# Output projection in four uses of one token tile, projection products regrouped, small exponential moved

## The chip, the cores and the metric

The kernel runs on one core of a Trainium2 chip. The metric is the device time of one execution in microseconds, as the median of several runs. TensorE (PE) multiplies, ScalarE (ACT) computes Ln and Exp, VectorE (DVE) does the elementwise work and the copies out of PSUM, GpSimd (POOL) only fills constants at the start, SyncE (SP) issues the DMAs. PSUM has eight banks of 128 x 512 fp32.

## The reference

One transformer layer on x of shape (8, 1024, 256), fp32, with 16 heads of 16 columns. Cut to what matters:

```python
xn = layernorm(x)
q, k, v = heads(xn @ Wq.T), heads(xn @ Wk.T), heads(xn @ Wv.T)
q, k, v = exp_map(q), exp_map(k), exp_map(v)        # tanh(|v|) * v / |v|
arg  = max(1 + 2c * |q_i - k_j|^2 / ((1 - c|q_i|^2) (1 - c|k_j|^2)), 1 + eps)
w    = softmax(-beta * arccosh(arg) / sqrt(c), axis=-1)
o    = log_map(exp_map(w @ log_map(v)))
x    = x + concat(o) @ Wo.T
y    = layernorm(x) quantised to e4m3, @ kernel quantised to e4m3, in fp32
x    = x + (bf16(y) + bias)
```

## The kernel before

**Tiling.** The 8192 tokens are 16 groups G of 512 tokens (4 tiles of 128), two groups to a batch entry. For each query group the attention runs over 4 head groups of 4 heads and 8 key tiles: 32 steps s of one chunk, 512 steps in all. A chunk is 128 keys x 4 heads x 512 queries. In a step PE makes the distance products of the chunk (L1100, 8 matmul instructions a step, half of chunk n+1 and half of chunk n+2), ACT takes Ln of the chunk in PSUM (L1217) and Exp of the one before (L1224), PE multiplies the values by the weights (L1115). In the loop the order on ACT is Ln(n), Exp(n-1), and after them, in one step of a group, the small exponential (L529, 128x128) for the projection. The distance products have two halves of a ring in six PSUM banks; those for chunk n+1, second half, wait until Ln(n) has emptied its banks (semaphore `freed`), and Ln(n+1) waits for them (`d_rdy`).

**Open units.** For each unit of 4 chunks a flag says whether some distance may reach the bound 1/eps. Where it is set, DVE first writes the bounds (L1285) and multiplies them into the distances (L1294), and ACT takes Ln of that (L1212). With these inputs three units are open: steps 4 to 7 of group 5, 20 to 23 of group 8, 12 to 15 of group 15.

**Side work in bank 7.** The other work runs beside the attention, in one PSUM bank (7), one use after another: PE fills it, DVE copies it out, and only then may PE fill it again (`b7_filled`, `b7_copied`). Uses of the projection of a coming group: X 0, 1 (x transposed), M 0 to 7 (products with Wq, Wk, Wv, two for a token tile, 128x384), R 0 to 7 (rows of q and k transposed), A 0, 1 (largest value over the tokens, transposed twice; the opens flags come from it). Uses of the finish of a group whose attention is over: T 0, 1 (attention output transposed), W (output projection), Q (quantised rows transposed), Y 0, 1 (second product). S turns the sums of a head group and DVE normalises them (`normalise`, L1308 to L1312), in steps 2, 10, 18 and 26 of a group.

**The order.** It is written out by hand. `PROJECT_USES` and `FINISH_USES` give each use a slot and a half: 0 is whole ahead of the products with the values, 1 whole behind them, `BOTH` a half ahead and a half behind. The projection of group n, from 3 on, runs in group n-2 with slot k at step k-4 (`EARLY`), the finish of group n in group n+1 with slot k at step k. Group 2 (`SECOND_USES`), group 1 (`FIRST_USES`) and the finish of group 14 (`SHORT_USES`, `SHORT_SLOTS`, in group 15) have tables of their own. The functions `vector`, `scalar` and `sync` of both stages hold, by slot, the work of DVE, ACT and SP. On every engine the instructions stand in one queue in this order. In a step DVE first does the copies of the step's uses, then the vector slots of the finish and of the projection. In a step with no use of bank 7 PE multiplies a constant into it instead (L1138, `keep_busy`, two instructions ahead of the values and two behind); the step `BARE` has neither.

**Names of the slots before.** Projection: squares and their sums in slots 9, 11, 14, 17; reciprocal roots by Newton steps (L267 to L269) in 18 and 19, at the end of 19 `nrm` (L596); values scaled in 20; the small exponential in 21 (ACT) and its use in 21 to 23 (DVE); rows scaled (L554) in 24. Finish: slots 3 to 8 for the output's length, 21 and 22 for mean and variance of the layernorm, 23 to 26 normalising and quantising, 28 and 32 the rest; SP loads x in slot 2 and stores the result in slot 33.

Of the kernel before, what the change touches and what calls it, by code (L numbers as in the profile page):

```python
# [303 lines left out]
def project_stage(nc, ctx, g, a, uses):  # L304


    def sb(name, shape, dt=F32):
# [222 lines left out]

    def first_vector(v, n, step):
# [7 lines left out]
        vector(v, n, 18, step)  # L539
        vector(v, n, 19, step)  # L540
        if n == 0:
            v.wait_ge(zeroed, ZEROED)
        vector(v, n, 20, step)
        vector(v, n, 21, step)
        vector(v, n, 22, step)
# [1084 lines left out]
```

## Time and profile before

| what | value |
|---|---|
| median of 3 runs | 1992.58 us (1991.73 to 1993.07) |
| profiled execution, its own time | 1994.49 us |
| its span, first to last instruction | 1992.7 us |
| busy: ACT / PE / DVE | 1869.9 us (94%) / 1788.6 us (90%) / 1142.9 us (57%) |
| Ln of closed chunks (L1217) | x500, mean 1911 ns, idle before 35.5 us, of it 31.6 waiting for PE L1100 |
| Exp (L1224) | x512, mean 1949 ns, idle before 0.3 us |
| Ln of open chunks (L1212) | x12, idle before 28.4 us, of it 28.3 waiting for DVE L1294 |
| mean granted clock of PE | 0.972 of full speed |

Busy times overlap: ACT's instructions are listed with a part of their wait in its queue, so start times tell more than durations. Clock 1 means that PE ran at its upper level, 2.4 GHz.

### The profile page before, as it was taken

How to read it: one execution, taken by the hardware profiler on the slowest of the kernel's cores; microseconds unless marked ns; L12 is line 12 of the kernel's file. 1: busy time of each engine (PE TensorE's matmuls, PEld its weight loads, DVE VectorE, ACT ScalarE, POOL GpSimd, SP SyncE). 2: the span in 40 equal slices, each digit the busy share in tenths (PEclk: the TensorE clock that was granted, in tenths of full speed). 3: DMA queues.
4: the chain of work that ended last, by engine and by line, in shares of the span. 5: the costliest groups of instructions: out<-in, count | busy, mean ns of one | idle time of the engine just before them, and what ended most of it. 6: DMA issues, size and time to landing. Idle time of an engine off the chain costs nothing.

```text
span 1992.7 us, 29554 instructions
## 1 busy us (share of the span) xinstructions
PE 1788.6 (90%) x10713; PEld 603.1 (30%) x10713; DVE 1142.9 (57%) x2825; ACT 1869.9 (94%) x1094; POOL 12.8 (1%) x35
## 2 busy tenths in 40 slices
PE   7988989989898798989998898998989899899897
PEld 4322222323232232322322223232322223233234
DVE  7454565655656656565656647565565656323436
ACT  4889999999999799999998999999999999999883
POOL 2000000000000000000000000000000000000000
PEclk9799999999999899999999899999999999999889
DMA  1314213141312213132040321314131131411110
GB/s 56 112 49 144 54 54 103 42 134 43 112 44 78 77 44 112 43 101 75 23 134 22 110 67 44 112 43 134 40 107 52 56 90 43 123 43 53 33 33 23
DMA packets 112953, 142.54 MB, mean 72 GB/s; under 512 B 35691, under 2 KB 61548, under 8 KB 112748
## 3 DMA queue, kind: packets, MB, share of 16 engines
q1 hardware_dynamic: 112748, 140.13, 22.6%
q8 instruction: 89, 1.46, 0.3%
q14 instruction: 116, 0.95, 0.2%
HBM read 85.07 MB, written 55.05 MB: 70 GB/s over the span
## 4 chain that ended last, share of the span: by engine, by line
ACT 54%; PE 24%; issue 14%; DVE 4%; ACTq 3%; DMA 0%; DVEq 0%; SPq 0%
ACT U L1217 28%; ACT U L1224 26%; PE ps L1100 8%; PE ps L401 6%; PE ps L1115 5%; ACTq L1265 2%; PE ps L695 2%; DVE U L1294 1%; PE ps L1138 1%; PE ps L406 1%; PE ps L1142 1%; DVE U L1285 1%; DVE rows L554 0%; DMA U<-in_L_attn_W_o_dram 0%; ACT e L529 0%
## 5 line engine op out<-in xcount | busy, mean ns | idle before, releaser
L1224 ACT ACTIVATE U<-U 128x2048 f32<-128x2048 f32 x512 | 997.1, 1949 | 0.3
L1217 ACT ACTIVATE U<-ps 128x2048 f32<-128x2048 f32 x500 | 955.7, 1911 | 35.5 <-PE ps L1100 31.6
L1100 PE MATMUL ps<-q_T,k_T 18*128 18x512 f32 x4096 | 632.5, 652 | 133.0 <-ACT U L1217 107.7
L1115 PE MATMUL ps<-U,vals 128*32 128x512 f32 x4096 | 560.4, 620 | 29.4 <-ACT U L1224 28.9
L1100 PEld LDWEIGHTS ps<-q_T,k_T 18*128 18x128 f32 x4096 | 195.9, 187 | 356.8 <-ACT U L1217 296.4
L401 PE MATMUL ps<-wT,xnT 128*128 128x384 f32 x512 | 232.0, 545 | 4.9 <-DVEq L1318 2.5
L490 DVE COPY qkv<-ps 128x384 f32<-128x384 f32 x112 | 62.4, 557 | 243.7 <-PE ps L401 243.6
L1115 PEld LDWEIGHTS ps<-U,vals 128*32 128x32 f32 x4096 | 81.7, 109 | 205.4 <-ACT U L1224 159.2
L401 PEld LDWEIGHTS ps<-wT,xnT 128*128 128x128 f32 x512 | 81.1, 194 | 197.0 <-issue 132.4
L1138 PE MATMUL ps<-woT,ident 128*128 128x256 f32 x340 | 121.8, 441 | 3.8 <-DVEq L1318 3.6
L406 PE MATMUL ps<-ident,rows 128*128 128x128 f32 x512 | 107.2, 308 | 4.9 <-DVE rows L554 2.4
L406 PEld LDWEIGHTS ps<-ident,rows 128*128 128x128 f32 x512 | 55.1, 146 | 176.4 <-issue 114.5
L1138 PEld LDWEIGHTS ps<-woT,ident 128*128 128x128 f32 x340 | 52.0, 193 | 145.2 <-issue 116.0
L1300 DVE COPY OTs<-ps 128x512 f32<-128x512 f32 x64 | 43.8, 684 | 88.0 <-PE ps L1115 75.3
L498 DVE COPY q_T<-ps 128x512 f32<-128x512 f32 x60 | 41.5, 691 | 90.9 <-PE ps L406 90.3
L500 DVE COPY k_T<-ps 128x512 f32<-128x512 f32 x60 | 41.5, 691 | 62.8 <-PE ps L406 60.8
L695 PE MATMUL ps<-woT,fi_ocT 128*128 128x256 f32 x240 | 68.6, 409 | 0.0
L1308 DVE TENSOR_REDUCE den<-ps 128x16 f32<-128x256 f32 x64 | 27.2, 424 | 58.2 <-PE ps L1124 57.2
L695 PEld LDWEIGHTS ps<-woT,fi_ocT 128*128 128x128 f32 x240 | 41.0, 191 | 51.8 <-issue 37.3
L723 DVE TENSOR_TENSOR fi_x<-fi_xt,ps 128x512 f32<-128x512 f32 x30 | 20.6, 688 | 61.9 <-PE ps L695 61.9
L587 DVE TENSOR_TENSOR sqr<-qkv 128x768 f32<-128x768 f32 x56 | 53.3, 953 | 2.4
L588 DVE TENSOR_REDUCE ss<-sqr 128x48 f32<-128x768 f32 x56 | 53.4, 953 | 1.9
(209 smaller groups left out, 1179.6 us busy)
## 6 DMA issues: line engine op xcount, KB each, us to landing
rqb<-q_scratch SPq DMA_DIRECT2D x64, 1024.0 KB, 5.6
q_scratch<-q_T SPq DMA_DIRECT2D x16, 1024.0 KB, 4.5
k_scratch<-k_T SPq DMA_DIRECT2D x16, 1024.0 KB, 6.8
v_scratch<-vals SPq DMA_DIRECT2D x16, 768.0 KB, 9.6
fi_xt<-in_L_attn_x_dram SPq DMA_DIRECT2D x17, 512.0 KB, 6.0
xt<-in_L_attn_x_dram SPq DMA_DIRECT2D x15, 512.0 KB, 6.7
out_dram<-fi_x SPq DMA_DIRECT2D x15, 512.0 KB, 4.6
rk_scratch<-rk SPq DMA_DIRECT2D x16, 32.0 KB, 12.5
```

Of the source, the lines that this page charges most:

```text
L401: ins = pe.matmul(bank[:, 0:384], xnT[:, dc, t * P:(t + 1) * P], g.wT[:, dc, half * 384:(half + 1) * 384], start=dc == 0, stop=dc == 1)
L406: ins = pe.transpose(bank[:, t * P:(t + 1) * P], rows[:, qk, t, hg * HPG:(hg + 1) * HPG, :].rearrange("p h r -> p (h r)"), g.ident[:, :])
L490: v.tensor_copy(qkv[:, t, 24 * half:24 * (half + 1), :].rearrange("p h d -> p (h d)"), bank[:, 0:384]).then_inc(a.b7_copied, 1)
L587: step(v.tensor_tensor(sqr[:, :], src, src, ALU.mult))
L588: step(v.tensor_reduce(ss[:, t, :], sqr[:, :].rearrange("p (h d) -> p h d", d=DH), AX.X, ALU.add))
L695: ins = pe.matmul(bank[:, a * D:(a + 1) * D], ocT[:, dc, t * P:(t + 1) * P], g.woT[:, dc, :], start=dc == 0, stop=dc == 1)
L1100: ins = pe.matmul(g.ps[:, 2 * pair + i, :], a.k_T[HB * h:HB * h + RD, b % 2, hg, kt * P:(kt + 1) * P], a.q_T[HB * h:HB * h + RD, G % 3, hg ...
L1115: ins = pe.matmul(g.ps[HB * h:HB * h + VW, 6, :], a.vals[:, b % 2, kt, (hg * HPG + h) // 2, DH * (h % 2):DH * (h % 2) + VW], U[:, n % RING ...
L1138: pe.matmul(g.ps[:, 7, 0:D], g.ident[:, :], g.woT[:, 0, :], start=True, stop=True)
L1217: act.activation(U[:, n % RING].rearrange("p b n -> p (b n)"), chunk(n), ACT.Ln, scale=-2.0 / EPS, bias=1.0).then_inc(freed, 1)
L1224: act.activation(U[:, n % RING], U[:, n % RING], ACT.Exp, scale=exponent).then_inc(exp_done, 1)
L1300: v.tensor_copy(OTs[:, :], g.ps[:, 6, :]).then_inc(ot_done, 1)
```

## The change

1. Output projection: W 0 and W 1, each with two token tiles, become W 0 to W 3 with one tile each (slots 15, 16, 17, 19). The residual addition is by one tile, and `bn_stats` follows tile by tile in the same slots.
2. The products M 0 to M 7 of groups from 3 on: slots 7, 8, 9, 10, 12, 13, 15, 16 become 7, 8, 10, 11, 12, 15, 16, 17. T 0 moves from 13 to 9.
3. The Newton steps are spread over slots 19, 20, 21 (`nrm` at the end of 21), the small exponential moves from slot 21 to 22 on ACT, what uses it from 21, 22, 23 to 23, 24, 25, the scaling of the rows from 24 to 25 (q) and 26 (k), the values' scaling from 20 to 35 (31 for group 2).
4. R and A move by one slot; A 0, A 1 and R 4 are new in the second half of slots 28, 31 and 30. Steps S and R in the tables of groups 1 and 2 no longer share step 10, and R 0 of group 2 stands in the second half of step 26.
5. The stores of q, k, v, rk go from slot 34 to 36, the output's from 33 to 34. The finish of group 14 uses the common table with the slots packed from step 10 on.
6. `BARE` is step 5 instead of 7.

```diff
-PROJECT_SLOTS = 35
-FINISH_SLOTS = 34
+PROJECT_SLOTS = 37
+FINISH_SLOTS = 35
 PROJECT_USES = {("X", 0): (4, BOTH), ("X", 1): (5, BOTH),
-                ("M", 0): (7, BOTH), ("M", 1): (8, BOTH), ("M", 2): (9, BOTH), ("M", 3): (10, BOTH),
-                ("M", 4): (12, BOTH), ("M", 5): (13, BOTH), ("M", 6): (15, BOTH), ("M", 7): (16, BOTH),
-                ("R", 0): (25, BOTH), ("R", 1): (26, BOTH), ("R", 2): (27, 0), ("A", 0): (27, 1),
-                ("R", 3): (28, BOTH), ("R", 4): (29, BOTH), ("R", 5): (31, 0), ("A", 1): (31, 1),
+                ("M", 0): (7, BOTH), ("M", 1): (8, BOTH), ("M", 2): (10, BOTH), ("M", 3): (11, BOTH),
+                ("M", 4): (12, BOTH), ("M", 5): (15, BOTH), ("M", 6): (16, BOTH), ("M", 7): (17, BOTH),
+                ("R", 0): (26, BOTH), ("R", 1): (27, BOTH), ("R", 2): (28, BOTH), ("A", 0): (28, 1),
+                ("R", 3): (29, BOTH), ("R", 4): (30, 1), ("R", 5): (31, BOTH), ("A", 1): (31, 1),
                 ("R", 6): (32, BOTH), ("R", 7): (33, BOTH)}
-FINISH_USES = {("T", 0): (13, BOTH), ("T", 1): (14, BOTH), ("W", 0): (15, BOTH), ("W", 1): (17, BOTH),
+FINISH_USES = {("T", 0): (9, BOTH), ("T", 1): (14, BOTH), ("W", 0): (15, BOTH), ("W", 1): (16, BOTH),
+               ("W", 2): (17, BOTH), ("W", 3): (19, BOTH),
                ("Q", 0): (30, BOTH), ("Y", 0): (31, 0), ("Y", 1): (31, 1)}
-SHORT_USES.update({("Q", 0): (28, BOTH), ("Y", 0): (30, 0), ("Y", 1): (30, 1)})
-BARE = 7
-SHORT_SLOTS = {23: (23, 24), 24: (25, 26), 25: (27, 28), 26: (29,), 27: (30, 31), 28: (32,), 29: (33,), 30: (), 31: ()}
+BARE = (5,)
+SHORT_SLOTS = {10: (10, 11, 12, 13), 11: (14,), 12: (15,), 13: (16,), 14: (17, 18), 15: (19,), 16: (20, 21), 17: (22,),
+               18: (23,), 19: (24,), 20: (25,), 21: (26, 27), 22: (28, 29, 30), 23: (31, 32), 24: (33,), 25: (34,),
+               26: (), 27: (), 28: (), 29: (), 30: (), 31: ()}
 FIRST_USES = {("A", 0): (2, 0), ("R", 4): (2, 0), ("A", 1): (2, 0), ("R", 5): (3, BOTH), ("R", 6): (6, BOTH),
-              ("R", 7): (11, BOTH), ("R", 0): (14, BOTH), ("R", 1): (17, BOTH), ("R", 2): (19, BOTH),
-              ("R", 3): (20, BOTH)}
+              ("R", 7): (14, BOTH), ("R", 0): (17, BOTH), ("R", 1): (19, BOTH), ("R", 2): (20, BOTH),
+              ("R", 3): (21, BOTH)}
-SECOND_USES.update({("R", 0): (25, BOTH), ("R", 1): (26, BOTH), ("R", 2): (27, 0), ("A", 0): (27, 1), ("R", 3): (28, 0),
-                    ("R", 4): (28, 1), ("R", 5): (29, BOTH), ("R", 6): (30, 0), ("A", 1): (30, 1), ("R", 7): (31, BOTH)})
+SECOND_USES.update({("M", 2): (9, BOTH), ("M", 4): (12, BOTH), ("M", 5): (13, BOTH), ("M", 6): (15, BOTH), ("M", 7): (16, BOTH),
+                    ("R", 0): (26, 1), ("R", 1): (27, 0), ("A", 0): (27, 1), ("R", 2): (28, 0), ("R", 3): (28, 1),
+                    ("R", 4): (29, BOTH), ("R", 5): (30, 0), ("A", 1): (30, 1), ("R", 6): (31, 0), ("R", 7): (31, 1)})
...
         elif kind == "W":
-            for a in halves(part, range(2)):
-                t = 2 * i + a
-                for dc in range(2):
-                    ins = pe.matmul(bank[:, a * D:(a + 1) * D], ocT[:, dc, t * P:(t + 1) * P],
-                                    g.woT[:, dc, :], start=dc == 0, stop=dc == 1)
+            for dc in halves(part, range(2)):
+                ins = pe.matmul(bank[:, 0:D], ocT[:, dc, i * P:(i + 1) * P], g.woT[:, dc, :],
+                                start=dc == 0, stop=dc == 1)
...
     def scalar(act, n, k):
-        if k == 21:
+        if k == 22:
...
-        if k == 19:
-            newton(v, step, ss[:, :, :], y[:, :, :], y2[:, :, :], 2)
+        if k == 20:
+            newton(v, step, ss[:, :, :], y[:, :, :], y2[:, :, :], 1)
+        if k == 21:
+            newton(v, step, ss[:, :, :], y[:, :, :], y2[:, :, :], 1)
             v.tensor_tensor(nrm[:, :, :], ssqk, yqk, ALU.mult).then_inc(n_rdy, 1)
...
-        if k == 21:
-            v.wait_ge(b7_copied, uses.after(("W", n, 1)))
-            for t in range(GT):
-                step.mark(v.bn_stats(stats[:, t, :], x1[:, t, :]))
+        if k in (15, 16, 17, 19):
+            t = {15: 0, 16: 1, 17: 2, 19: 3}[k]
+            v.wait_ge(b7_copied, uses.after(("W", n, t)))
+            step.mark(v.bn_stats(stats[:, t, :], x1[:, t, :]))
+        if k == 20:
```

## Rows read from the trace of the kernel before

**Rows 1.** Timeline of group 3 and the first step of group 4, ACT: start, us, what.

```profile
415.58 1.96 ACT L1217 ACTIVATE U<-ps 128x2048 f32<-128x2048 f32 x1
419.13 1.97 ACT L1217 ACTIVATE U<-ps 128x2048 f32<-128x2048 f32 x1
...
437.06 1.88 ACT L1217 ACTIVATE U<-ps 128x2048 f32<-128x2048 f32 x1
...
440.82 1.88 ACT L1217 ACTIVATE U<-ps 128x2048 f32<-128x2048 f32 x1
...
530.71 1.97 ACT L1217 ACTIVATE U<-ps 128x2048 f32<-128x2048 f32 x1
```

**Rows 2.** Timeline, group 3, steps 15 to 18; in brackets the idle time before.

```profile
473.12 1.88 ACT L1217 ACTIVATE U<-ps 128x2048 f32<-128x2048 f32 x1
...
475.77 1.14 PE L1100 MATMUL ps<-q_T,k_T 18*128 18x512 f32 x8
...
476.94 1.88 ACT L1217 ACTIVATE U<-ps 128x2048 f32<-128x2048 f32 x1
...
479.09 1.14 PE L1100 MATMUL ps<-q_T,k_T 18*128 18x512 f32 x8
...
480.51 0.39 ACT L529 ACTIVATE e<-nrm,sc 128x128 f32<-128x128 f32 x1
...
480.81 1.87 ACT L1217 ACTIVATE U<-ps 128x2048 f32<-128x2048 f32 x1
```

**Rows 3.** Timeline, group 3, steps 23 and 24: A 0 and transpositions.

```profile
502.26 1.90 ACT L1217 ACTIVATE U<-ps 128x2048 f32<-128x2048 f32 x1
...
503.74 0.28 PE L411 MATMUL ps<-ident,amax 128*32 128x128 f32 x1 [0.23 <-DVE q_T L498]
...
504.21 1.24 PE L1100 MATMUL ps<-q_T,k_T 18*128 18x512 f32 x8 [0.19 <-ACT U L1217]
...
507.48 0.69 DVE L498 COPY q_T<-ps 128x512 f32<-128x512 f32 x1 [1.61 <-PE ps L406]
```

**Rows 4.** Timeline, DVE, group 3 and the last tokens of the kernel.

```profile
478.49 0.36 DVE L269 SCALAR_TENSOR_TENSOR y<-y 128x192 f32<-128x192 f32 x1
...
478.89 0.29 DVE L596 TENSOR_TENSOR nrm<-ss,y 128x128 f32<-128x128 f32 x1
...
1966.76 0.42 DVE L886 TENSOR_TENSOR fi_x<-fi_xt,ps 128x256 f32<-128x256 f32 x1 [0.70 <-PE ps L842]
1967.21 0.43 DVE L887 BATCH_NORM_STATS2 fi_stats<-fi_x 128x6 f32<-128x256 f32 x1
```

**Rows 5.** Timeline, group 3, step 26: the sums.

```profile
514.78 0.49 DVE L1312 TENSOR_TENSOR on<-ps,den 128x128 f32<-128x128 f32 x2
514.91 1.24 PE L1100 MATMUL ps<-q_T,k_T 18*128 18x512 f32 x8 [0.70 <-ACT U L1217]
```

**Rows 6.** ACT's waits in 98:180, 1855:1872 and 1925:1950: us, times, longest.

```profile
ACT U L1217 <- PE ps L1100: 9.7, 3, 5.9
...
ACT U L1217 <- PE ps L1100: 3.7, 2, 2.7
...
ACT U L1217 <- PE ps L1100: 4.0, 3, 1.9
```

**Rows 7.** Timeline, group 8, ahead of its open unit.

```profile
1075.60 1.88 ACT L1217 ACTIVATE U<-ps 128x2048 f32<-128x2048 f32 x1
...
1081.69 1.67 DVE L1285 TENSOR_SCALAR U<-rqb,rk 128x512 f32<-128x512 f32 x4
```

**Rows 8.** Windows: length, busy PE, PEld, DVE, ACT, POOL, granted clock, DMA.

```profile
400.00:500.00 100.00, 92.45 (x572) 29.75 (x571) 57.95 (x141) 99.70 (x57) 0.00 (x0) 1.00 0.27 88
```

**Rows 9.** Timeline, PE, three places with idle time.

```profile
102.94 1.65 PE L401 MATMUL ps<-wT,xnT 128*128 128x384 f32 x2 [2.50 <-DVEq L1318]
...
1855.80 1.81 PE L1100 MATMUL ps<-q_T,k_T 18*128 18x512 f32 x8 [0.70 <-ACT U L1217]
...
1954.19 1.07 PE L1115 MATMUL ps<-U,vals 128*32 128x512 f32 x8 [1.44 <-ACT U L1224]
```

More of the change, by code:

```diff
@@ L366, in sync @@
             sp.dma_start(xt[:, :, :], g.x_g[n + 1]).then_inc(x_in, 16)
-        if k == 34:
+        if k == 36:
             b, u = n // 2, n % 2
@@ L538, in first_vector @@
         step(v.tensor_scalar(ss[:, :, :], ss[:, :, :], EPS * EPS, None, ALU.max))
[L539 to L545, printed above, removed]
+        for k in (19, 20, 21, 35):
+            if k == 35 and n == 0:
+                v.wait_ge(zeroed, ZEROED)
+            vector(v, n, k, step)
+        vector(v, n, 23, step)
+        vector(v, n, 24, step)
         if n == 1:
             v.wait_ge(p_filled, len(FIRST_FILLS))
-        vector(v, n, 23, step)
+        vector(v, n, 25, step)
         scale_rows(v, n, (1, 0) if n == 0 else (1,))
@@ L582, in vector @@
             ins.then_inc(xn_rdy, 1)
-        if k in (9, 11, 14, 17):
-            t = {9: 0, 11: 1, 14: 2, 17: 3}[k]
+        if k in (9, 12, 16, 18):
+            t = {9: 0, 12: 1, 16: 2, 18: 3}[k]
             v.wait_ge(a.b7_copied, uses.after(("M", n, 2 * t + 1)))
@@ L590, in vector @@
                 step(v.tensor_scalar(ss[:, :, :], ss[:, :, :], EPS * EPS, None, ALU.max))
-        if k == 18:
+        if k == 19:
             root_guess(v, step, ss[:, :, :], y[:, :, :])
             newton(v, step, ss[:, :, :], y[:, :, :], y2[:, :, :], 1)
-        if k == 19:
-            newton(v, step, ss[:, :, :], y[:, :, :], y2[:, :, :], 2)
+        if k == 20:
+            newton(v, step, ss[:, :, :], y[:, :, :], y2[:, :, :], 1)
+        if k == 21:
+            newton(v, step, ss[:, :, :], y[:, :, :], y2[:, :, :], 1)
             v.tensor_tensor(nrm[:, :, :], ssqk, yqk, ALU.mult).then_inc(n_rdy, 1)
-        if k == 20:
+        if k == (31 if n == 2 else 35):
+            step = first or Steps(v, g_steps, 2 * (n - 2))
             step(v.tensor_scalar(vg[:, :, :], y[:, :, 2 * H:], g.ZS, 1.0, ALU.mult, ALU.min))
@@ L607, in vector @@
                                 ALU.mult).then_inc(v_rdy, 1)
-        if k == 21:
+        if k == 23:
             v.wait_ge(e_rdy, n + 1)
@@ L621, in vector @@
             step(v.reciprocal(rp[:, :, :], a4[:, :, :]))
-        if k == 23:
+        if k == 25:
             if n >= 4:
@@ L629, in vector @@
             v.tensor_reduce(amax[:, :], a4[:, :, :].rearrange("p t h -> p h t"), AX.X, ALU.max).then_inc(amax_rdy, 1)
-        if k == 24:
-            scale_rows(v, n, (1, 0))
-        assert first or step.n == OWN.get(k, 0), (k, step.n)
+            if n >= 2:
+                scale_rows(v, n, (0,))
+        if k == 26:
+            scale_rows(v, n, (1,))
+        assert first or k in (31, 35) or step.n == OWN.get(k, 0), (k, step.n)
     p = Shared()
@@ L670, in sync @@
             if n >= 1:
-                sp.wait_ge(steps_v, PER * (n - 1) + sum(count for slot, count in OWN.items() if slot <= 28))
+                sp.wait_ge(steps_v, PER * (n - 1) + sum(count for slot, count in OWN.items() if slot <= 27))
             sp.dma_start(xt[:, :, :], g.x_g[n]).then_inc(f_in, 16)
-        if k == 33:
+        if k == 34:
             sp.wait_ge(res_rdy, n + 1)
@@ L722, in copy @@
                     v.wait_ge(res_out, 16 * n)
-            v.tensor_tensor(x1[:, two, :].rearrange("p t d -> p (t d)"),
-                            xt[:, two, :].rearrange("p t d -> p (t d)"), bank, ALU.add).then_inc(b7_copied, 1)
+            v.tensor_tensor(x1[:, i, :], xt[:, i, :], bank[:, 0:D], ALU.add).then_inc(b7_copied, 1)
         elif kind == "Q":
@@ L962, in in_step @@
                     found.append(("S", x // HG, x % HG))
-            found += [(kind, n, i) for n, k in finished(G, s) for kind, i in at(finish_uses(n), k, half)]
+            found += [(kind, n, i) for n, k in finished(G, s) for kind, i in at(FINISH_USES, k, half)]
             found += [(kind, n, i) for n, k in projected(G, s) for kind, i in at(project_uses(n), k, half)]
@@ L1054, in _ @@
                 project.first_sync(sp, 2)
-                project.sync(sp, 0, 34)
+                project.sync(sp, 0, 36)
                 load_rq(0)
@@ L1061, in _ @@
                     if n == 21:
-                        project.sync(sp, 1, 34)
+                        project.sync(sp, 1, 36)
                     if n == N - 3:
@@ L1163, in _ @@
                     both = [(kind, m, i) for m, k in projected(G, s) for kind, i in begun(project_uses(m), k)]
-                    both += [(kind, m, i) for m, k in finished(G, s) for kind, i in begun(finish_uses(m), k)]
+                    both += [(kind, m, i) for m, k in finished(G, s) for kind, i in begun(FINISH_USES, k)]
                     if G == 0:
@@ L1172, in _ @@
                         use(*key, 0)
-                    unused = n > 2 and s != BARE and not in_step(G, s, 0) + in_step(G, s, 1)
+                    unused = n > 2 and s not in BARE and not in_step(G, s, 0) + in_step(G, s, 1)
                     if unused:
```

28 lines of the change are left out of this document (12 added, 16 removed).

## The prediction

> **What bounds the kernel now.** I read the page first, for who is busy and who ends the waits, then the timeline of ScalarE (ACT) alone, taking differences of start times, since the listed durations overlap and grow while its queue is full. In the page ACT is the bound: 512 Ln and 512 Exp, and the wait it has most is for the distance products, 31.6 us of the run (the table above). In the timeline, step 96 (group 3, step 0) starts at 415.58 and step 128 at 530.71 [rows 1]: 115.13 us for 32 steps. Unhindered steps start 3.555 apart (415.58 and 419.13); thirty-two of them are 113.8, so a steady group loses only 1.4 us. Over the run 512 x 3.555 = 1820 us; the rest of the 1992.7 us span is what lies ahead of and behind the loop, 14 x 1.4 us in groups 1 to 14, and waits in group 0, in group 15 and in the three units whose flag is open. The profiled execution took 1994.49 us, 1.8 over its span; the median of the runs is 1992.58. I add differences to the median.
>
> Where do the 1.4 us go? The reader should see in [rows 2] how PE's lateness reaches ACT: PE starts a step's distance products at 475.77 and the next Ln starts at 476.94, 1.17 later. It can't start them before the Ln of that step is through, 1.95 us after its start (502.26 and 504.21, where PE waited for just that) [rows 3]. That leaves 3.56 - 1.95 - 1.17 = 0.44 us by which PE may be late for nothing. The use of the output projection in step 111 makes PE start its next products 2.65 us after the Ln (473.12, 475.77) [rows 2]: the allowance is used up, and the next Ln comes 3.82 us after the last (473.12, 476.94) instead of 3.56. The small exponential adds 0.30: 480.51 to 480.81. In a run of four projection products each step past the second is 3.76 long (437.06 to 440.82) [rows 1]: 0.2 lost in each.
>
> **The change, part by part.** Steps are s, slots k; for the projection of a later group s = k - 4, for the finish s = k.
>
> *Output projection in four.* A half of a use is now two instructions of 256 columns instead of four, like the filler's half. The filler step is 475.77 to 479.09, 3.32 us [rows 2], under 3.56: no loss. Gain 0.3 us a group. The additions are four of 0.42 us on DVE [rows 4] instead of two of twice the width, hidden by its idle half, as are the statistics that move with them.
>
> *Products in pairs.* Runs of 4, 2, 2 become 2, 3, 3. By 0.2 for each past the second: 0.4 before, 0.4 after. Nothing. The fullest DVE slot (the copy of R 0, the ten small operations of slot 22, one scaling) comes to a little over a step but is followed by a lighter one: nothing.
>
> *The small exponential.* Its input nrm moves from slot 19 to 21, it only from 21 to 22. So one step lies between them where two did. DVE's slot s=17 now holds: the addition of W 2, which can begin some 5.4 us after the Ln of 17 (a copy behind half a transposition begins 5.22 after the Ln of its step, 502.26 to 507.48 [rows 3]; half a W is 0.2 longer); addition and hand-over 0.45, statistics 0.35, three Newton operations of 0.40 (478.49 to 478.89 is one), nrm 0.29 [rows 4]. Sum 7.7. ACT reaches the exponential 3.57 after the Ln of its step [rows 2], which is 7.13 after the Ln of 17. It waits 0.6 us, and every Ln queued behind it too. Bounds: 0 if DVE is 0.6 quicker than its rows, 1.0 if the copy meets a late PE.
>
> *A 0 behind R 2, A 1 behind R 5.* Both use the same bank. Before, R 2 was whole in the first half and the products with the values lay between. Now R 2 ends in the second half and A 0 can't start until DVE has copied it, 0.69 and a hand-over of 0.06. With the copy at 507.48 A 0 would start at 508.23, end 0.28 later (as at 503.74), and the distance products would start at 508.51; the Ln after them at 509.68 instead of 505.81 + 3.56 = 509.37 (505.81 is 502.26 + 3.55): 0.3 us [rows 3]. A 1 stands the same way behind R 5: 0.3. Bounds 0 and 0.75 each.
>
> *R 4 behind the sums.* In s=26 the sums are turned first, DVE normalises, R 4 stands behind the values. In [rows 5] PE is through with the values at 514.2 (0.70 ahead of 514.91), but DVE with the last of the normalising at 515.3 (514.78 + 0.49) and a hand-over of 0.1: the quantising work of slot 25 held it, and that stays. So PE idles 1.2 us, R 4 takes some 0.6, and the distance products start near 516.0 instead of 514.9: 1.1 late less the allowance of 0.44. Cost 0.7, bounds 0.3 and 0.9.
>
> So groups 1 to 13 get 0.6 + 0.3 + 0.3 + 0.7 - 0.3 = 1.6 us each, 21 us.
>
> *What moves without cost.* The values are scaled at slot 35 (s=31), where DVE had only the copies of Y, and first used at step 4 of the next group, so four steps in hand. The four stores of q, k, v, rk go out at slot 36 (s=0 of the next group) instead of 34; on SP's queue stand behind them the two loads of x, wanted more than ten steps later, and the broadcast load at the next s=4, whose data only open units read. The output store moves one step, to s=2, and its wait for the result holds up the same queue by less than a step. If that cover were gone, each late step of SP would cost 3.6 us once.
>
> *Group 0.* The sums no longer share s=10 with M 3, nor s=26 with a transposition ahead of the values. These were ACT's waits of 5.9 and 3.8, together 9.7 us [rows 6]. Gone but for 0.7: -9.
>
> *Group 15.* Finish of group 14 ends four steps earlier: Q no longer waits for a late DVE; 4.0 us [rows 6]. The step without filler moves from 7 to 5; behind it the clock fell, 3.7 us [rows 6], though the same step of group 14 brought no wait; I count two thirds of it, 2.4. Against it, W 0 to W 3 now fall in the open unit, where DVE is the bound: 3 x 0.5 more. Sum -5.
>
> *Open units.* In group 8 DVE began the bounds of the first open chunk 6.1 us after the Ln of step 275 (1075.60, 1081.69) [rows 7]. Now W 3 is copied there only at 5.45 and 3.0 us of work follow: +2.4. Group 5 -0.5, group 14 -0.4 (W).
>
> Sum without the clock: 21 - 9 - 5 + 1.5 = +8.5 us: 2001.
>
> **The clock.** This decides the size. PE had its upper level, 2.4 GHz, all through 400 to 500 [rows 8]. Elsewhere it fell to 1.2 GHz, and ahead of that PE had idled: 2.50 us in one piece ahead of 102.94 (behind it two product instructions take 1.65 us) [rows 9], and twice in one step ahead of 1855.80, 0.70 us the second time, where the eight distance instructions take 1.81 us [rows 9] instead of the 1.14 at 475.77 [rows 2]. In steady groups there are idle pieces of 0.70 as well, one in a step of the sums [rows 5], and it did not fall [rows 8]. In one place 1.44 us of idle left it up (the values at 1954.19 still take 1.07) [rows 9]. The change makes, in each of groups 1 to 13, one idle of 0.7 (step of the sums) + 0.3 (exponential) + 0.6 (its wait) = 1.55 us at s=18 to 19, one of 1.2 at s=26, and two of 0.75. By the three rows (2.50 fell, 1.44 did not, 0.70 twice in a step fell) I take it to fall about once a group. A fall costs 3.7, 3.8 (of the 9.7) and 4.0 us in [rows 6], part of it the wait that led to it, already counted: 3.0. 13 x 3.0 = 39. Bounds: none, and two falls a group, 78.
>
> The Trainium skill (TensorE: Matmul & The Clock Gate, "A second HAM failure mode: psum-queue depth-cycling") says that short idles between groups of matmuls, often enough, make the clock swing between its levels; by that rule alone every group would fall, by the steady rows alone (0.70 us idle, no fall) none.
>
> Forecast: 1992.6 + 8.5 + 39 = 2040 us.
>
> **The rivals.**
> A. Clock falls once in most groups: 2040, from 2018 (0.45 falls a group) to 2070 (1.7). Chance 0.5.
> B. Waits come, clock stays: 2001 (1996 to 2012). For it: 1.44 us without a fall, and single pieces of 0.70 harmless throughout. Against: 1.55 is longer than any piece that is known to leave it up. Chance 0.25.
> C. Faster: the four waits are mostly covered, that is the exponential's input is ready in time and DVE frees the bank within PE's 0.44 us. Then the groups give 13 x -0.3, with group 0 and 15: -4 -9 -5 +1.5 = -16, 1976; with a third of the waits left 1984. It decides below 0.9 us of waits a group (13 x 0.9 = 12, less the 12.5 gained elsewhere). For it: DVE is busy only 58 of 100 us [rows 8], so its slots may end earlier than the sums say. Against: each wait is a sum of hand-overs that the trace shows. Chance 0.17.
> D. No visible change, gains and losses cancelling, 1989 to 1997: 0.08.
>
> **How the numbers follow.** 0.2% is 4 us, about what a measurement of this kernel can tell. Slower: A 0.5, B 0.24 = 0.74. Same: D 0.08 and a sliver of B, 0.09. Faster: C 0.17. The range goes from 1990, into the cases where the gains win, to 2065, short of two falls in every group: it leaves out most of C and the top of A, 0.2.
>
> **What would show it.** Small exponential: in groups 1 to 13 ACT's wait for nrm 0.6 us at s=18, so 13 such waits in the chain of waits; none refutes that step. A 0, A 1: PE waiting 0.75 for DVE's copies; R 4: PE waiting about 1.1 for the normalising. Steps of W at 3.56 apart. Granted clock: mean well below 0.97, with about 13 stretches at the lower level in groups 1 to 13, most behind s=18; if it stays 0.97 or more, B or C. Group 0: no wait of 5.9 near step 12. Group 15: no wait at Q. The prediction is wrong if the groups are no longer than 115.1 us, which the starts of every 32nd Ln show.

## The result, and the profile after

The changed kernel takes 2031.37 us (median of 6 runs, 2022.14 to 2037.63) where the kernel before takes 1992.15 (6 runs, 1986.07 to 1993.07): ratio 1.0201, 95% interval 1.0175 to 1.0228. It is 39 us slower; 2040 was forecast. The profiled execution took 2031.51 us with a span of 2029.7 us, 37.0 more than the span before. Its mean granted clock is 0.959 (0.972 before).

I read it as before: starts of Ln on ACT. Timeline of group 3 after, its first step and that of group 4:

```profile
409.06 1.89 ACT L1218 ACTIVATE U<-ps 128x2048 f32<-128x2048 f32 x1
...
525.73 1.89 ACT L1218 ACTIVATE U<-ps 128x2048 f32<-128x2048 f32 x1
```

116.67 us where it was 115.13 [rows 1]: 1.54 more; 1.6 was forecast. Group 6 is just as long; in these two the clock stays up. The waits after, of ACT and then of PE (total us, times, longest):

```profile
ACT U L1218 <- PE ps L1101: 53.3, 56, 4.6
...
ACT e L531 <- DVE nrm L599: 9.3, 14, 1.7
```

```profile
PE ps L408 <- DVEq L1319: 17.8, 14, 1.7
...
PE ps L413 <- DVE q_T L500: 14.3, 13, 1.5
PE ps L416 <- DVE k_T L502: 11.2, 15, 0.8
```

All four forecast waits are there: e for nrm, R 4 behind the sums (L408 for DVE's queue), A 0 (L413), A 1 (L416). In the timeline after, group 3, steps 18 and 19:

```profile
473.65 1.89 ACT L1218 ACTIVATE U<-ps 128x2048 f32<-128x2048 f32 x1
...
477.92 0.40 ACT L531 ACTIVATE e<-nrm,sc 128x128 f32<-128x128 f32 x1 [0.58 <-DVE nrm L599]
478.23 1.86 ACT L1218 ACTIVATE U<-ps 128x2048 f32<-128x2048 f32 x1
...
480.14 1.24 PE L1101 MATMUL ps<-q_T,k_T 18*128 18x512 f32 x8 [1.68 <-ACT U L1218]
```

ACT stands 0.58 us for nrm; Ln follows Ln after 4.58, 1.02 over a free step, of which 0.32 was there before. PE then has idled 1.68 us in one piece. Steps 25 to 29 of the same group:

```profile
499.57 1.91 ACT L1218 ACTIVATE U<-ps 128x2048 f32<-128x2048 f32 x1
...
502.16 0.28 PE L413 MATMUL ps<-ident,amax 128*32 128x128 f32 x1 [0.96 <-DVE q_T L500]
...
503.54 1.88 ACT L1218 ACTIVATE U<-ps 128x2048 f32<-128x2048 f32 x1 [0.27 <-PE ps L1101]
...
507.12 1.86 ACT L1218 ACTIVATE U<-ps 128x2048 f32<-128x2048 f32 x1
...
509.62 0.66 PE L408 MATMUL ps<-ident,rows 128*128 128x128 f32 x4 [1.28 <-DVEq L1319]
...
511.39 1.88 ACT L1218 ACTIVATE U<-ps 128x2048 f32<-128x2048 f32 x1 [0.60 <-PE ps L1101]
511.65 1.07 PE L1116 MATMUL ps<-U,vals 128*32 128x512 f32 x8
...
513.87 0.18 PE L416 MATMUL ps<-ident,amax_r 32*1 32x32 f32 x1 [0.79 <-DVE k_T L502]
...
515.05 1.88 ACT L1218 ACTIVATE U<-ps 128x2048 f32<-128x2048 f32 x1
```

A 0 costs 503.54 - 499.57 - 3.555 = 0.42, R 4 costs 511.39 - 507.12 - 3.555 = 0.71, A 1 costs 515.05 - 511.39 - 3.555 = 0.11. (These two are much the same in all quiet groups, but for 1.09 behind R 4 in group 10; A 0 costs between 0.22 and 1.06 in groups 1 to 13.) Now the same place in group 7:

```profile
1001.38 1.88 ACT L1218 ACTIVATE U<-ps 128x2048 f32<-128x2048 f32 x1 [0.60 <-PE ps L1101]
1001.64 1.90 PE L1116 MATMUL ps<-U,vals 128*32 128x512 f32 x8
...
1007.07 1.88 ACT L1218 ACTIVATE U<-ps 128x2048 f32<-128x2048 f32 x1 [2.01 <-PE ps L1101]
```

Steps 26 and 27 lose the same as in group 3 (0.02 and 0.71 us), but here the values take 1.90 us where they took 1.07: the clock has fallen. The next Ln comes 5.69 after the last. The windows after (groups 9 to 13, then group 15; the columns are those of [rows 8], the granted clock is third from the end) say it in sum:

```profile
1156.90:1753.56 596.66, 535.72 (x3249) 167.81 (x3248) 342.05 (x851) 576.09 (x326) 0.00 (x0) 0.97 0.24 74
1867.39:1988.09 120.70, 107.22 (x626) 35.15 (x624) 58.33 (x125) 111.58 (x63) 0.00 (x0) 0.96 0.14 45
```

Before, groups 9 to 13 took 575.86 us at 1.00 and group 15 took 125.22 at 0.89 (up to the last Ln).

**Where the 37 us come from**, by the starts of every 32nd Ln, before and after: group 0 ends at 185.28 and 173.45 (-11.8: it is 9.7 shorter, 137.96 and 128.22, and its first Ln 2.1 earlier, 47.32 and 45.23); groups 1 to 13 together +54.9, that is 13 x 1.54 = 20.0, the first step of group 8's open unit +3.5, and the other 31, which stand in the groups where the clock falls; group 14 -0.9; group 15 -4.5. Sum +37.7; behind the last Ln 0.7 comes back.

Outside the open units the granted clock falls 14 times in groups 1 to 13 after, and never before: once at step 19 or 20 in groups 2, 4, 5, 7, 11, 12 and 13, and at steps 28 to 30 once in groups 7, 8, 9, 11 and 12 and twice in 13. (A fall here is a stretch at the lower level, 1.2 GHz.) 31 / 14 = 2.2 us each.

### The profile page after: what moved, and what is told of

Read it like the earlier page. It is cut to its first block, busy times and chain, and to the rows that moved or that the text cites. A ratio compares the mean times of both kernels' runs of the same rounds, so it can differ in the third digit from the quotient of the medians.

```text
span 2029.7 us, 29437 instructions
## 1 busy us (share of the span) xinstructions
PE 1795.7 (88%) x10645; PEld 588.3 (29%) x10645; DVE 1144.3 (56%) x2855; ACT 1873.5 (92%) x1094; POOL 12.5 (1%) x35
## 4 chain that ended last, share of the span: by engine, by line
ACT 34%; PE 33%; DVE 17%; issue 12%; ACTq 2%; DVEq 1%; DMA 0%; SPq 0%
ACT U L1218 18%; ACT U L1225 16%; PE ps L1101 11%; PE ps L1116 9%; PE ps L403 7%; PE ps L408 2%; PE ps L699 2%; ACTq L1266 2%; DVE q_T L500 2%; DVE rows L555 1%; DVE U L1295 1%; DVE fi_ocT L775 1%; DVE fi_xb L767 1%; DVEq L1365 1%; DVE rp L615 1%
## 5 line engine op out<-in xcount | busy, mean ns | idle before, releaser
L1225 ACT ACTIVATE U<-U 128x2048 f32<-128x2048 f32 x512 | 989.3, 1934 | 0.3
L1101 PE MATMUL ps<-q_T,k_T 18*128 18x512 f32 x4096 | 638.8, 657 | 128.8 <-ACT U L1218 91.5
L1116 PE MATMUL ps<-U,vals 128*32 128x512 f32 x4096 | 571.4, 631 | 19.0 <-ACT U L1225 17.4
L403 PE MATMUL ps<-wT,xnT 128*128 128x384 f32 x512 | 227.9, 537 | 1.6 <-ACT xnT L464 1.6
L408 PE MATMUL ps<-ident,rows 128*128 128x128 f32 x512 | 112.4, 315 | 35.9 <-DVEq L1319 17.8
L408 PEld LDWEIGHTS ps<-ident,rows 128*128 128x128 f32 x512 | 55.4, 148 | 230.9 <-issue 124.1
L727 DVE TENSOR_TENSOR fi_x<-fi_xt,ps 128x256 f32<-128x256 f32 x60 | 25.3, 421 | 127.7 <-PE ps L699 127.7
L1139 PE MATMUL ps<-woT,ident 128*128 128x256 f32 x272 | 96.9, 439 | 0.0
L699 PE MATMUL ps<-woT,fi_ocT 128*128 128x256 f32 x240 | 89.6, 457 | 0.0
L1139 PEld LDWEIGHTS ps<-woT,ident 128*128 128x128 f32 x272 | 41.3, 191 | 113.7 <-issue 101.8
L1213 ACT ACTIVATE U<-U 128x2048 f32<-128x2048 f32 x12 | 22.9, 1911 | 36.5 <-DVE U L1295 36.5
```

What stands on the lines that cost most here:

```text
L403: ins = pe.matmul(bank[:, 0:384], xnT[:, dc, t * P:(t + 1) * P], g.wT[:, dc, half * 384:(half + 1) * 384], start=dc == 0, stop=dc == 1)
L408: ins = pe.transpose(bank[:, t * P:(t + 1) * P], rows[:, qk, t, hg * HPG:(hg + 1) * HPG, :].rearrange("p h r -> p (h r)"), g.ident[:, :])
L699: ins = pe.matmul(bank[:, 0:D], ocT[:, dc, i * P:(i + 1) * P], g.woT[:, dc, :], start=dc == 0, stop=dc == 1)
L1101: ins = pe.matmul(g.ps[:, 2 * pair + i, :], a.k_T[HB * h:HB * h + RD, b % 2, hg, kt * P:(kt + 1) * P], a.q_T[HB * h:HB * h + RD, G % 3, hg ...
L1116: ins = pe.matmul(g.ps[HB * h:HB * h + VW, 6, :], a.vals[:, b % 2, kt, (hg * HPG + h) // 2, DH * (h % 2):DH * (h % 2) + VW], U[:, n % RING ...
L1139: pe.matmul(g.ps[:, 7, 0:D], g.ident[:, :], g.woT[:, 0, :], start=True, stop=True)
```

## The experiments

The profiled executions of all kernels side by side. Lengths of groups in us by Ln starts; falls are those of groups 1 to 13 outside the open units of groups 5 and 8. Only the ratio rests on several executions. The other columns are one execution each, and they differ from run to run: the one of e2 (2010.96 us) lies 10 us below the median of its kernel, that of e4 (1989.28) 6 below, that of e3 (2045.03) 8 above.

| kernel | ratio to before, interval | group 0 | groups 1-4 | 9-13 | falls | group 15 |
|---|---|---|---|---|---|---|
| before | 1 | 138.0 | 460.6 | 575.9 | 0 | 125.2 |
| changed | 1.0201 (1.0175 to 1.0228) | 128.2 | 471.1 | 596.7 | 14 | 120.7 |
| e1_exp_later | 1.0088 (1.0055 to 1.0121) | 129.5 | 472.0 | 590.5 | 9 | 120.7 |
| e2_r4_beside_r3 | 1.0154 (1.0121 to 1.0187) | 128.2 | 466.6 | 588.6 | 8 | 120.4 |
| e3_a_behind_values | 1.0225 (1.0187 to 1.0263) | 131.8 | 478.1 | 597.1 | 24 | 126.5 |
| e4_all_three | 1.0019 (0.9997 to 1.0042) | 131.1 | 461.6 | 578.7 | 1 | 120.4 |
| g5_fill_idle | 1.0161 (1.0132 to 1.019) | 135.1 | 468.8 | 591.4 | 8 | 120.7 |
| h2_exp_earlier | 1.0093 (1.0066 to 1.012) | 138.4 | 467.3 | 583.6 | 2 | 119.9 |
| g6_w_alone | 0.9935 (0.9912 to 0.9958) | 138.4 | 459.1 | 573.8 | 0 | 115.6 |
| g7_group0_tables | 0.9968 (0.9952 to 0.9984) | 131.2 | 460.6 | 576.0 | 0 | 124.1 |
| g8_parts_alone | 0.993 (0.9909 to 0.9951) | 128.8 | 459.2 | 573.9 | 0 | 121.5 |
| h1_w_and_group0 | 0.9907 (0.9887 to 0.9926) | 125.0 | 459.1 | 573.8 | 0 | 120.5 |

**1. The small exponential one slot later.** The changed kernel with

```diff
     def scalar(act, n, k):
-        if k == 22:
+        if k == 23:
```

> The changed kernel with the small exponential one slot later still (23 instead of 22 on ACT), nothing else. Theory (the wait for nrm idles PE, and that idle lets the clock fall): ACT's waits for nrm, 14 of 9.3 us together, are gone, the step behind s=18 is 3.56 long again and the next 3.86 instead of 4.58, and the clock no longer falls behind s=19 of groups 1 to 13 (8 falls in the changed kernel); 9 us of waits and about 12 us behind the falls come back: 2010 us. Falls at s=28 stay. Rival (the falls at s=20 have another cause, such as W 3 and the fuller DVE slots there): the wait goes, the falls stay, 2022 us. Rival (ACT's wait is covered elsewhere): no change, 2031.

Measured 2010.35 us (5 runs, 2003.45 to 2014.62), before on that chip 1989.4. The wait for nrm is gone from groups 1 to 13, and with it every fall at steps 19 and 20 (seven; the eight above are a miscount); 0.29 is left of the step. Falls at steps 26 to 30 are left, nine of them (five at 28), more than the seven of the changed kernel, and groups 1 to 4 gain nothing: 472.0 against 471.1.

**2. R 4 beside R 3.** The changed kernel with

```diff
-                ("R", 3): (29, BOTH), ("R", 4): (30, 1), ("R", 5): (31, BOTH), ("A", 1): (31, 1),
+                ("R", 3): (29, 0), ("R", 4): (29, 1), ("R", 5): (31, BOTH), ("A", 1): (31, 1),
```

> The changed kernel with R 3 whole ahead of the values and R 4 whole behind them in slot 29 (s=25), so that R 4 no longer stands behind the sums of s=26. Theory: the 0.7 us behind s=27 go in each of groups 1 to 13 (9 us), PE's wait for the normalising (17.8 us in all) is gone, and with it the falls at s=28 to 30 (7 in the changed kernel, some 17 us): 2005 us. Rival (the falls there belong to the wait of A 1 at s=27): only the 9 us go and A 1 keeps its falls, 2022 us. Rival (R 4 beside R 3 makes a wait for R 3's copy in its place): 2028.

Measured 2020.71 us (5 runs, 2010.96 to 2022.81). Less than the theory's gain. Waits of PE:

```profile
PE ps L408 <- DVE q_T L500: 8.4, 11, 1.0
```

The wait for the normalising is gone, but R 4 behind the values now waits for the copy of R 3, as A 0 does for that of R 2: 0.50 lost instead of 0.71. What did go, in this execution, are the falls at steps 28 to 30, all of them. Those at 19 and 20 are there in five groups, and three at 23 and 26 have come.

**3. A 0 and A 1 with their R whole ahead of the values.** The changed kernel with

```diff
-                ("R", 0): (26, BOTH), ("R", 1): (27, BOTH), ("R", 2): (28, BOTH), ("A", 0): (28, 1),
-                ("R", 3): (29, BOTH), ("R", 4): (30, 1), ("R", 5): (31, BOTH), ("A", 1): (31, 1),
+                ("R", 0): (26, BOTH), ("R", 1): (27, BOTH), ("R", 2): (28, 0), ("A", 0): (28, 1),
+                ("R", 3): (29, BOTH), ("R", 4): (30, 1), ("R", 5): (31, 0), ("A", 1): (31, 1),
```

> The changed kernel with R 2 and R 5 whole ahead of the values, so that A 0 and A 1 no longer wait for a copy made after the values. Theory: the 0.2 to 1.0 us behind s=25 and the 0.1 behind s=28 go, 13 x 0.5 = 6.5 us, and PE's waits of 14.3 us (A 0) and 11.2 us (A 1) shrink to below 5 each; the falls at s=28 become fewer, not none: 2018 to 2025 us. Rival (these waits are inside PE's allowance and cost nothing by themselves): 2031.

Measured 2036.98 us (4 runs, 2030.82 to 2045.03): a miss. Waits of PE, and the timeline of group 3 (step 25):

```profile
PE ps L413 <- DVE q_T L500: 20.2, 13, 1.9
```

```profile
507.92 1.88 ACT L1218 ACTIVATE U<-ps 128x2048 f32<-128x2048 f32 x1 [0.59 <-PE ps L1101]
509.99 0.69 DVE L500 COPY q_T<-ps 128x512 f32<-128x512 f32 x1 [1.25 <-issue]
...
510.74 0.28 PE L413 MATMUL ps<-ident,amax 128*32 128x128 f32 x1 [1.28 <-DVE q_T L500]
```

R 2's copy begins no sooner (2.07 us after the Ln; 1.84 in the changed kernel, 501.41 against 499.57), so A 0 still waits for it, and longer. The idle marked "issue" ahead of the copy is no wait for PE, which is through with R 2 at 508.46. Step 24 begins a unit of 4 chunks, and there DVE's queue reads the unit's flag and branches on it (L1365, L1366) before it gets to the copy. These instructions don't count as busy; the chain of waits shows them from 508.78 to 509.90, after the quantising. In the changed kernel they stand at the same place (L1365 begins at 500.5). The clock is low in 24 places here, at least once in each of groups 1 to 13; these groups together are only 4.6 us longer than in the changed kernel, group 0 is 3.6 and group 15 5.8 longer. Putting R ahead is no cure while the copy itself is late.

**4. All three edits together.**

> All three placements undone at once (exponential at 23, R 3 and R 4 in slot 29, R 2 and R 5 ahead of the values); the four uses of W, the products' slots, the tables of groups 0 and 15 stay as changed. Theory: a steady group takes 114.7 us instead of 116.7 to 122 (before the change 115.1), no fall of the clock in groups 1 to 4, 6, 7 and 9 to 14; with group 0 shorter by 12, group 15 by 4.5, group 14 by 0.9 and group 8 longer by 3.4: 1974 us, faster than the kernel before by 0.9%. Rival (what is left of the change, the fuller DVE slots and the runs of three products, brings losses that the three waits hid): 1985 to 1995.

Measured 1995.08 us (10 runs, 1984.14 to 1998.51): level with the kernel before. That is the rival's figure; the theory's 1974 was a miss by 21. Windows of it, groups 1 to 4 and 9 to 13:

```profile
178.50:640.13 461.63, 418.55 (x2602) 133.47 (x2600) 275.15 (x693) 459.23 (x261) 0.00 (x0) 1.00 0.24 77
1133.05:1711.78 578.73, 524.68 (x3252) 167.19 (x3250) 342.16 (x851) 574.17 (x327) 0.00 (x0) 1.00 0.24 75
```

The clock stays up but for one fall (group 12). Steady groups are 115.3 to 115.7 long, still above 115.13, since R 4 and A 0 keep 0.5 and 0.1 to 0.5. That is 0.8 a group over the 114.7 of the theory, 10 us, and neither the fuller slots nor the runs of three products are behind it, as the rival had it. Group 0 ends 5.0 us later than in the changed kernel (178.50, 173.45); the last 6 us lie between this execution and the median. The 9.5 us that the changed kernel has over this one in groups 1 to 4, and 18 in groups 9 to 13, are waits and the falls that come with them.

**5. Is it the idle of PE that lets the clock fall?** The changed kernel, its wait for nrm kept, and two filler instructions put where PE stands idle:

```diff
                     if unused:
                         keep_busy(first_use[n])
+                    if s == 18 and 1 <= G < LAST - 1:
+                        keep_busy(first_use[n] + 1)
```

> The changed kernel with one instruction pair of filler (a constant into bank 7) added behind the products with the values in step 18 of groups 1 to 13, where ScalarE waits for nrm. The wait itself stays, so the direct losses (1.5 us a group) stay. Theory (the idle of TensorE makes its clock fall): none of the 7 falls that the changed kernel has at steps 19 and 20 of groups 2, 4, 5, 7, 11, 12, 13 (2.35 us each in groups 2 and 4, about 1 in 7, 11, 12 and 13, 3.8 in 5: 12 us together) comes, those at steps 28 to 30 remain: about 2019 us where the changed kernel has 2031, granted clock 0.965. Rival 1 (the fall follows from the wait, not from TensorE's idle): falls as before, 2031. Rival 2 (the filler makes the distance products late): 13 times 0.3 more, 2035.

Measured 2023.33 us (4 runs, 2015.49 to 2026.64), before on that chip 1992.55. Its timeline, group 3, steps 18 and 19:

```profile
487.01 0.70 PE L1139 MATMUL ps<-woT,ident 128*128 128x256 f32 x2 [1.01 <-DVEq L1321]
487.68 1.24 PE L1101 MATMUL ps<-q_T,k_T 18*128 18x512 f32 x8
```

The idle piece is 1.01 us instead of 1.68, and the distance products are not later. The step still costs ACT 1.02 in every one of groups 1 to 13, and no group has a fall at steps 19 and 20 (seven before the edit). Those at 26 to 30 are left, 8 of them. Groups 1 to 13 are 17.2 us shorter together; group 0, which the edit doesn't touch, is 6.9 longer. So the wait alone doesn't bring the fall; PE's idle in it does. The other executions agree: where the wait is there without filler, falls at steps 19 and 20 come in 7, 5 and 11 groups (changed kernel, experiments 2 and 3); where it is gone (1 and 4) or filled (this one), in none.

**6. One wait alone, in the kernel before.** Small exponential one slot earlier, and one Newton step one slot earlier so that the slot of nrm is as full as in the changed kernel:

```diff
     def scalar(act, n, k):
-        if k == 21:
+        if k == 20:
...
         if k == 18:
             root_guess(v, step, ss[:, :, :], y[:, :, :])
-            newton(v, step, ss[:, :, :], y[:, :, :], y2[:, :, :], 1)
+            newton(v, step, ss[:, :, :], y[:, :, :], y2[:, :, :], 2)
         if k == 19:
-            newton(v, step, ss[:, :, :], y[:, :, :], y2[:, :, :], 2)
+            newton(v, step, ss[:, :, :], y[:, :, :], y2[:, :, :], 1)
```

> The kernel before with its small exponential one slot earlier and one Newton step of DVE moved a slot ahead, so that one step lies between nrm and the exponential, as in the changed kernel, and nothing else. Theory: ScalarE waits for nrm 0.6 to 0.8 us in groups 1 to 13, 9 us; that wait is also an idle piece of TensorE, so its clock falls at steps 17 to 19 in four to seven of them, 1 to 2.4 us each, 8 us more: 2009 us where the kernel before has 1992. Rival: one wait by itself lets no clock fall, since in the changed kernel four waits and less filler come together: 2001, granted clock as before (0.972). Rival 2: no wait, 1992.

Measured 2009.29 us (4 runs, 2002.02 to 2010.58), before on that chip 1987.09. The forecast time, but not by its sum. Timeline, group 3, step 16:

```profile
482.75 0.40 ACT L529 ACTIVATE e<-nrm,sc 128x128 f32<-128x128 f32 x1 [1.24 <-DVE nrm L596]
...
484.97 1.24 PE L1100 MATMUL ps<-q_T,k_T 18*128 18x512 f32 x8 [1.09 <-ACT U L1217]
```

The wait is 1.24 us, twice what was meant (the addition of two tiles stands ahead of it, 0.69 us), and costs 1.27 a group, 16.5 in 13. The clock falls in only 2 of 13 groups. Here PE has filler ahead of and behind the values in the same step; its idle piece is 1.09, and it falls seldom. Groups 1 to 13 are 21.3 us longer, more than the 17 of the forecast; that the time fits is partly luck, for group 15, by falls at other places, is 5.4 shorter (119.9, 125.2).

**7. Parts of the change alone.** Output projection in four uses with its statistics tile by tile, in the kernel before (the hunks for W, `bn_stats` and the table, as in the change):

```diff
-FINISH_USES = {("T", 0): (13, BOTH), ("T", 1): (14, BOTH), ("W", 0): (15, BOTH), ("W", 1): (17, BOTH),
+FINISH_USES = {("T", 0): (13, BOTH), ("T", 1): (14, BOTH), ("W", 0): (15, BOTH), ("W", 1): (16, BOTH),
+               ("W", 2): (17, BOTH), ("W", 3): (19, BOTH),
```

> The kernel before with the output projection alone in four uses of one token tile, statistics tile by tile. Theory: 0.26 us less at step 16 of groups 1 to 14, 3.6 us in all, and up to 2 us more in group 8, where the fourth use stands in the step ahead of the open unit; nothing else: 2 to 4 us faster than the kernel before, ratio 0.998 to 0.999, no fall of the clock outside groups 0, 5, 8 and 15. Rival: four copies of 0.42 us in place of two make DVE late in steps 17 to 19, or four uses leave TensorE idle often enough for falls at step 20: 5 to 20 us slower.

Measured 1978.63 us (6 runs, 1971.47 to 1983.08): 13 us faster by the ratio, more than the 2 to 4 forecast. Steady groups are 114.78 long, 0.35 shorter. Group 8 is 1.7 shorter, not longer: its open unit's first step costs 1.1 more, a later one 1.4 less, and the two behind that 0.3 and 0.7 less. Group 5, whose open unit ends in a longer fall, is 4.0 longer, so groups 1 to 13 gain only 1.9 together. Another 2.1 lie ahead of the first Ln (45.25, 47.32), where the edit changes nothing. Group 15 is 9.6 us shorter: of its falls at steps 8, 12, 15 and 26 only the one at 15 is left, against a new one in group 14 that costs 1.2.

The new tables of group 0 in the kernel before:

```diff
-              ("R", 7): (11, BOTH), ("R", 0): (14, BOTH), ("R", 1): (17, BOTH), ("R", 2): (19, BOTH),
-              ("R", 3): (20, BOTH)}
+              ("R", 7): (14, BOTH), ("R", 0): (17, BOTH), ("R", 1): (19, BOTH), ("R", 2): (20, BOTH),
+              ("R", 3): (21, BOTH)}
...
-SECOND_USES.update({("R", 0): (25, BOTH), ("R", 1): (26, BOTH), ...
+SECOND_USES.update({("M", 3): (11, BOTH), ("R", 0): (25, BOTH), ("R", 1): (26, 1), ...
```

> The kernel before with the new tables of group 0 alone (R 7 to R 3 of group 1 at steps 14, 17, 19, 20, 21; M 3 of group 2 at slot 11, R 1 of group 2 behind the values). Theory: the two waits of 5.9 and 3.8 us go, and 0.7 comes back: 9 us faster, ratio 0.9955, group 0 ends near 176 us where it ended at 185.3. Rival: the falls of the clock in group 0 move to another step (the changed kernel has one of 1.7 us at step 15) and half of it is given back: 5 us.

Measured 1983.98 us (12 runs, 1977.97 to 1990.07), 6.4 us by the ratio. The long wait at step 11 is gone (6.05 lost before, 0.02 now). The fall at the group's end is not: it comes a step earlier and costs 2.3 (steps 26 and 27) where it cost 4.2. Steps 6 to 9 lose 1.1 more.

Both, with filler in the bare step of group 15 and the finish of group 14 packed from step 9 on (the change packs it from step 10):

```diff
+SHORT_SLOTS = {9: (9, 10, 11, 12, 13), 10: (), 11: (14,), 12: (15,), 13: (16,), 14: (17, 18), 15: (19,), 16: (20, 21), ...
...
-                    unused = n > 2 and s != BARE and not in_step(G, s, 0) + in_step(G, s, 1)
+                    unused = n > 2 and (s != BARE or G == NG - 1) and not in_step(G, s, 0) + in_step(G, s, 1)
```

> The kernel before with four things of the change alone: output projection in four, the tables of group 0, the finish of group 14 packed from step 9 on, and filler in the bare step of group 15 only. The small exponential, R, A, M and T stay where they were. Theory: -4 (output projection), -9 to -12 (group 0), -5 (group 15), +2 to +3 (group 8): 16 to 18 us faster than the kernel before, ratio 0.991 to 0.992, steady groups 114.9 us long, no clock fall in them. Rival: the parts that are good alone need the moved slots (DVE has no room for the statistics) and falls appear in the steady groups: ratio 1.00 or more.

Measured 1974.98 us (6 runs, 1972.26 to 1981.58), ratio 0.993. Less than the sum of the parts. ACT's waits from 1810 to 1940, of this kernel and then of the one with the output projection alone:

```profile
ACT U L1212 <- DVE U L1294: 9.0, 4, 4.7
```

```profile
ACT U L1211 <- DVE U L1293: 2.0, 2, 1.4
```

Packing puts the uses W 0 to W 3 into the four open steps, where DVE sets the pace, and the unit waits 7 us longer for it. Not all of that need be the packing: the next kernel has none, and its unit waits 5.5 us, with a fall of the clock in it as here (step 12, here 11).

Both without the packing, with filler in step 7 of groups 14 and 15:

> The kernel before with the output projection in four, the new tables of group 0, and filler in step 7 of groups 14 and 15; the finish of group 14 keeps its old steps. Measured alone: output projection 13.9 us, tables of group 0 8.6 us. With the finish of group 14 packed as well the open unit of group 15 lost 10.6 us over its four steps, without it 3.5. Theory (the packing is a loss, and the two gains stand in different groups and add): 13.9 + 6.7 (what group 0 itself gained) + 1 (filler, the fall in group 14) = 21 us faster than the kernel before, ratio 0.989 to 0.990, span near 1970. Rival (the output projection's 13.9 us were luck of the falls in group 15, where 6 us of them lie): the falls at steps 8 and 26 of group 15 come back, 1977, ratio 0.993.

Measured 1969.01 us (6 runs, 1966.63 to 1973.77), before on that chip 1987.09: ratio 0.9907, 0.9887 to 0.9926, the best of the twelve. Falls at 12, 16 and 26 of group 15 have come (the rival was half right), and group 0 is the shortest of all. Against the packed version (0.9909 to 0.9951) the intervals overlap: packing goes with 3.5 us more of that wait in the open unit (9.0, 5.5), but that it costs in the whole is not settled.

## Why the prediction was right, point by point

**The mechanism held.** Rival A, waits of ACT and PE that bring about one fall a group, is what the trace shows; experiments 1, 4 and 5 show the links: without the wait for nrm no fall behind it, with only two shorter waits left (PE idle 1.02 and 0.75 us) one fall in 13 groups, with the wait and PE busier no fall. Rival B (waits come, clock stays) would have been 2001; no run is that case, but the profiled execution less its 31 us of clock is about 2000. Rival C is refuted by the quiet groups, which are longer. The forecast is 9 us high; term by term (forecast, measured):

- *Small exponential*: +0.6 a group, measured 1.02 - 0.32 = +0.7.
- *A 0*: +0.3, measured 0.42; A 1: +0.3, measured 0.11, since its copy begins 1.73 us after the Ln (511.39, 513.12) and its transposition takes 0.18 instead of the 0.28 of A 0. The row that I took for both was that of A 0.
- *R 4*: +0.7, measured 0.71; PE idles 1.28, forecast 1.2.
- *Output projection*: -0.3, measured -0.26 and another -0.1 in step 18. *Pairs of products*: 0, measured -0.1 (steps 5 to 14).
- Together +1.6 and +1.54: 21 against 20.0.
- *Clock*: 13 falls of 3.0 = 39 against 14 of 2.2 = 31. **This is the term that was mis-sized.** The number was right, though in nine groups, four with two or three, and not one in each, so that it is partly luck. The price was too high because it was taken from long falls: in the kernel before, those of group 15 at steps 8 and 26 last about 10 us at clock 0.50, and their steps lose 4.1 and 4.4. Of the 14 after, seven last about 3 us and cost 1.0 to 1.4 each, four about 7 us (2.3), one about 10 us (3.8) and two about 14 us (4.3). Half lie behind step 18, where I had most; the other half behind R 4, where PE idles 1.28.
- *Group 0*: -9, measured -9.7, and -2.1 ahead of it that belongs to no edit: over all these kernels the first Ln starts between 45.0 and 47.5, with old tables and new. Nor is the 9.7 firm: the six kernels with the changed tables have lengths of 128.2 to 135.1, three with the old 138.0 to 138.4, by where the clock fell.
- *Group 15*: -5, measured -4.5, by larger sums than thought, so the agreement is luck: the losses at steps 8 to 10, 16 to 18 and 26 to 28 went (4.1, 2.1 and 4.4 us), and the open unit gave 6.1 back (1.5 forecast); ACT's wait for DVE there is 9.0 us, 3.2 before.
- *Open units*: +1.5 (2.4 in group 8, -0.5 in group 5, -0.4 in group 14), measured +3.5, +0.2 and -0.9. The step in group 8:

```profile
1094.66 0.42 DVE L727 TENSOR_TENSOR fi_x<-fi_xt,ps 128x256 f32<-128x256 f32 x1 [4.31 <-PE ps L699]
...
1098.77 1.67 DVE L1286 TENSOR_SCALAR U<-rqb,rk 128x512 f32<-128x512 f32 x4 [1.12 <-issue]
```

DVE begins the bounds 9.55 us after the Ln of step 19 (1089.22), 6.1 before [rows 7]: the fourth W is copied 5.44 us after that Ln (5.45 forecast), and statistics and the first use of the exponential follow until 1097.64 (1097.36 + 0.28), 3.0 us, as forecast. The missing 1.1 us is the idle piece marked "issue" ahead of the bounds; before, DVE went into them without one. The chain of waits of the kernel after shows what fills it, the reading of the unit's flag and the branch on it (start, us, what):

```profile
1097.68 0.05 DVEq L1371
...
1097.98 0.30 DVEq L1365
...
1098.59 0.05 DVEq L1366
```

Before, the same reading (L1364, 1080.9 to 1081.5) ran while DVE was still at the last operations of slot 23, which nothing in its queue waits for. After, slot 23 (the first use of the exponential) stands there, and the queue waits for its last operation (L619, until 1097.64) before it goes on to the flag. The prediction has no term for this.

The Trainium skill (TensorE: Matmul & The Clock Gate, "A second HAM failure mode: psum-queue depth-cycling") says of one measured kernel that TensorE's short idles between groups of matmuls, frequent enough, make the clock swing. Taken as a rule for every such idle, it would have every group fall; nine of thirteen did, and one idle of 1.09 us a group (experiment 6) brought 2 falls in 13. So the traces agree in kind and not in every group: in group 3 an idle of 1.68 us in one piece left the clock up.

**Left open.** Which group falls is not decided by what its steps show: groups 2 and 3 start their Ln at the same distances, to 0.02 us, up to step 19, and only the clock of group 2 falls at step 20. Executions of one kernel spread over 15 us, and the clock goes with it: 2022.14 us had 0.965, 2037.63 and 2034.49 had 0.955.

## What to carry to other kernels

Price a wait on the bounding engine twice: its own length, and the idle that it leaves on TensorE, which here cost half as much again as all the waits (31 us against 20). Where such a wait can't be removed, an instruction or two of filler inside it takes away the second part (7 falls of 7 at that step). When one rewrite bundles several edits, run the parts: here the output projection in four and the tables of group 0, kept alone (with filler in one more step of groups 14 and 15), gain 18 us, while the whole change costs 39.

## What the runs showed that I had not expected

- Falls differ in price: about 1 us at step 20 of groups 7, 11, 12 and 13, 1.4 at step 28 of groups 11 to 13, and 4.3 at the same step of groups 7 and 8, over three steps, where the lower level lasted longer.
- The output projection in single tiles gave 13 us, three times what its steps are worth; most of it is in group 15, by falls that no longer came (9.6 us shorter), and the same edit with the tables of group 0 and filler in step 7 had the falls back (120.5). A part of its gain is thus fragile.
- Filler, which uses PE and computes nothing, made a kernel 8 us faster (2023.33 against 2031.37 by the medians; the ratios, 1.0161 and 1.0201, have intervals that touch), while ACT, the bounding engine, waited as long as before for its input.
